# The last projection of an attention and FFN kernel: eight products of blocks replaced by seven (Strassen's scheme in Winograd's form), with the weight forms kept in DRAM

## What is computed

```python
def reference(x, ctx, gate, up, down):           # x, ctx: 16 x 128 x 1024, f32
    q, k, v = layernorm(x), ctx, ctx             # 8 heads over the 128 channels
    kvs = einsum('bnhd,bnhe->bhde', softmax(k, over n), v)
    x = x + einsum('bnhd,bhde->bnhe', softmax(q, over d), kvs)
    h = layernorm(x)                             # 2048 tokens x 1024
    inter = silu(h @ Wg.T) * (h @ Wu.T)          # 2048 x 2752
    return x + inter @ Wd.T                      # 2048 x 1024
```

## Time and profile before

| | us |
|---|---|
| median of the runs | 1581.06 |
| the profiled execution | 1582.67 |
| its span in the profile | 1581.0 |
| PE busy, of the span | 1560.3 (99%) |
| ACT busy | 847.4 (54%) |
| DVE busy | 479.3 (30%) |
| POOL busy | 60.9 (4%) |
| DMA | 203.5 MB, mean 129 GB/s |

### The profile page before, as it was taken

How to read it: one execution, slowest core, us unless ns; L and a number is a source line. 1 busy time by engine, 2 the same in 40 slices (tenths; PEclk the granted TensorE clock), 3 DMA queues, 4 the chain that set the end, 5 groups by cost and what they waited for, 6 DMA issues and landing times.

```text
span 1581.0 us, 17409 instructions
## 1 busy us (share of the span) xinstructions
PE 1560.3 (99%) x7296; PEld 1297.2 (82%) x7296; DVE 479.3 (30%) x592; ACT 847.4 (54%) x865; POOL 60.9 (4%) x99
## 2 busy tenths in 40 slices
PE   7999999999999999999999999999999999999999
PEld 6888788888888888888888888888778888888887
DVE  6998321212212222112122122213422224322221
ACT  5777876666666677666666666773211114111110
POOL 3434000000000000000000000000000000000000
PEclk9999999999999999999999999999999999999999
DMA  6553443333334433333333344336663433443340
GB/s 207 170 171 120 158 124 112 113 103 111 93 104 117 120 114 112 100 114 111 104 111 95 100 120 120 114 104 200 226 235 120 150 138 112 150 144 113 143 148 28
DMA packets 96430, 203.51 MB, mean 129 GB/s; under 512 B 7520, under 2 KB 52576, under 8 KB 92512
## 3 DMA queue, kind: packets, MB, share of 16 engines
q1 hardware_dynamic: 96352, 202.41, 40.6%
HBM read 150.99 MB, written 51.38 MB: 128 GB/s over the span
## 4 chain that ended last, share of the span: by engine, by line
PE 92%; ACT 4%; DMA 2%; issue 1%; SPq 1%; DVE 0%; DVEq 0%; ACTq 0%
PE bank L945 20%; PE bank L946 20%; PE bank L947 20%; PE bank L998 9%; PE bank L1000 9%; PE bank L999 9%; PE bank L896 2%; PE bank L923 1%; PE bank L930 1%; PE bank L913 1%; DMA F<-inter_scratch 1%; ACT early L548 1%; SPq L385 1%; ACT F L582 1%; ACT F L567 1%
## 5 line engine op out<-in xcount | busy, mean ns | idle before, releaser
L945 PE MATMUL bank<-R 128*128 128x512 f32 x1376 | 535.9, 389 | 0.0
L946 PE MATMUL bank<-R 128*128 128x512 f32 x1376 | 535.8, 389 | 0.0
L947 PE MATMUL bank<-R 128*128 128x512 f32 x1376 | 535.7, 389 | 0.0
L527 ACT ACTIVATE F<-F 128x1024 f32<-128x1024 f32 x441 | 467.5, 1060 | 13.3
L947 PEld LDWEIGHTS bank<-R 128*128 128x128 f32 x1376 | 258.4, 188 | 53.6
L945 PEld LDWEIGHTS bank<-R 128*128 128x128 f32 x1376 | 258.4, 188 | 53.4
L946 PEld LDWEIGHTS bank<-R 128*128 128x128 f32 x1376 | 258.4, 188 | 53.4
L663 ACT CAST R<-F 128x2816 fp32r<-128x2816 f32 x30 | 76.7, 2557 | 347.5 <-PE bank L1004 321.7
L998 PE MATMUL bank<-R 128*128 128x512 f32 x642 | 250.2, 390 | 2.6 <-DVE R L844 2.6
L1000 PE MATMUL bank<-R 128*128 128x512 f32 x642 | 250.0, 389 | 0.0
L999 PE MATMUL bank<-R 128*128 128x512 f32 x642 | 250.0, 389 | 0.0
(11 more groups left out here) (75 smaller groups left out, 791.4 us busy)
## 6 DMA issues: line engine op xcount, KB each, us to landing
F<-inter_scratch SPq DMA_DIRECT2D x30, 1408.0 KB, 7.5
inter_scratch<-F SPq DMA_DIRECT2D x84, 256.0 KB, 2.4
F<-in_gu_codes SPq DMA_DIRECT2D x41, 512.0 KB, 3.9
F<-in_gu_scales SPq DMA_DIRECT2D x82, 256.0 KB, 3.9
F<-in_d_codes SPq DMA_DIRECT2D x22, 512.0 KB, 3.8
F<-in_d_scales SPq DMA_DIRECT2D x44, 256.0 KB, 3.9
wd_scratch<-F SPq DMA_DIRECT2D x22, 512.0 KB, 4.5
F<-in_x SPq DMA_DIRECT2D x16, 512.0 KB, 3.6
```

The lines of the kernel that those rows point to most:

```text
L527: nc.scalar.activation(y, y, ACT.Prelu, bias=bias, scale=scale, alpha=alpha).then_inc(bent, 1)
L945: pe.matmul(dst, hi, xh[:, tb, t, :], start=(t == 0), stop=False)
L946: pe.matmul(dst, hi, xl[:, tb, t, :], start=False, stop=False)
L947: i = pe.matmul(dst, lo, xh[:, tb, t, :], start=False, stop=(t == HT - 1))
```

## The change

The down projection for 20 of the 21 full chunks is done in 5 rounds (4 chunks each) of 8 groups (two token tiles each), 40 groups. A group multiplies a 2x2 arrangement of activation blocks A (128 tokens x 256) with a 2x2 arrangement of weight blocks B (256 x 512), and does it with seven products in place of eight. A product is two steps of three matmuls. The operands are four activation blocks or sums of them (S1 to S4) and B blocks or sums (T1 to T4):

```diff
@@ ScalarE, gate and up stage, after each silu_of(c, tb)
+            def form_hi(c, tb):
...
+                wait(act, form_stored, 16 * k)
+                nc.scalar.copy(form[0], src).then_inc(fh_ready, 1)
@@ VectorE, gate and up stage, in every second chunk
+            def t_forms(c):
...
+                sub(T1, B12, B11).then_inc(t_ready, 1)
+                sub(T3, B22, B12).then_inc(t_ready, 1)
...
+                sub(T2, B22, T1).then_inc(t_ready, 1)
...
+                sub(T4, B21, T2).then_inc(t_ready, 1)
@@ VectorE, gate and up stage, after each block_out(c, tb)
+            def form_lo(c, tb):
...
+                dve.wait_ge(fh_ready, k + 1)
+                sub(form[1], src, form[0].bitcast(F32)).then_inc(fl_ready, 1)
@@ SyncE at the turn
             store_block(FULL, 0, HALF)
+            for m in range(NM // 4):
+                load_y(m)
             store_block(FULL, 1, HALF)
...
             store_block(FULL, 3, HALF)
...
+            load_stage(1)
+            for m in range(NM // 4, NM):
+                load_y(m)
...
+            for g in range(NG):
+                r, m = g // NM, g % NM
+                if g + 2 < NG:
+                    load_stage(g + 2)
+                if r + 1 < NR and m < NP:
+                    sp.wait_ge(product_done, NP * r * NM + m + 1)
+                    load_w(r + 1, m)
...
@@ ScalarE, down stage
+            for s in range(2):
+                act.wait_ge(inter_stored[s], 16 * (2 * FULL + 4))
+            for g in range(NG):
+                r, m = g // NM, g % NM
+                snapshot(g, 0, 0, (s3_added, g), s1_ready)
+                if g + 1 < NG:
+                    hi_a(g + 1)
+                if r == NR - 1 and m == 0:
+                    for k in range(2):
+                        act.wait_ge(restw_in, 32)
+                        nc.scalar.copy(restw[k][0], restw_in_f[k]).then_inc(hrw_ready, 1)
+                    hi_rest(0)
+                snapshot(g, 1, 2, (s2_added, g), s2_ready)
+                if g + 1 < NG:
+                    hi_s(g + 1)
+                snapshot(g, 0, 4, (s1_added, g + 1), s3_ready)
...
@@ VectorE, down stage
+                elif g:
+                    x_add(g - 1, (product_done, NP * g))
+                s1_add(g)
+                if g + 1 < NG:
+                    s_forms(g + 1)
+                    lo_a(g + 1)
+                q1_add(g)
+                s2_add(g)
+                if not last:
+                    w_add(g, (product_done, NP * g + 4))
+                if g + 1 < NG:
+                    lo_s(g + 1)
...
+                s3_add(g)
+                if not last:
+                    q2_add(g, (product_done, NP * g + 6))
...
@@ TensorE, down stage
-                        pe.matmul(dst, h, wdh[:, k, :], start=(k == 0), stop=False)
-                        pe.matmul(dst, h, wdl[:, k, :], start=False, stop=False)
-                        i = pe.matmul(dst, l, wdh[:, k, :], start=False, stop=False)
...
+            def product(g, i, dst, stationary, start):
...
+                for k in range(2):
+                    h, l = (v[:, k * P:(k + 1) * P] for v in stationary)
...
+                last.then_inc(product_done, 1)
...
+                pe.wait_ge(la_ready, g + 1)
+                wait(pe, x_added, g - 1)
...
+                product(g, 0, x, a11, True)
+                pe.wait_ge(ls_ready, g + 1)
+                wait(pe, q2_added, g - 1)
...
+                product(g, 1, q, s3, True)
+                pe.wait_ge(s1_ready, g + 1)
...
+                product(g, 2, x, s2, False)
+                wait(pe, w_added, g - 1)
...
+                product(g, 3, w2, a12, True)
+                pe.wait_ge(s2_ready, g + 1)
...
+                product(g, 4, x, s1, False)
+                pe.wait_ge(q1_added, g + 1)
...
+                product(g, 5, q, a22, False)
+                pe.wait_ge(s3_ready, g + 1)
...
+                product(g, 6, x, s4, False)
+                if r == NR - 1:
+                    pe.wait_ge(lrw_ready, 2)
+                    pe.wait_ge(lr_ready, m + 1)
...
+                    rest(m, w2, 0, 0, True)
+                    rest(m, q, 1, 0, True)
+                    rest(m, x, 0, 1, True)
+                    wait(pe, z_added, m)
+                    rest(m, bankZ, 1, 1, False)
```

More of the change, by code:

```diff
@@ L201, in xattn_ffn, with wd_tile @@
[L201 to L203 removed]
+        B11, B12, B21, B22 = [v[:, h * WIDE:(h + 1) * WIDE] for v in wdt for h in range(2)]
+        T1, T2, T3, T4 = tform
+        FORMS = [(B11, 0), (B21, 3), (B22, 6), (T1, 4), (T3, 1), (T2, 2), (T4, 5)]
+        KINDS = (2, 0, 3, 1)
+        def wd_tile(c):
+            return 4 * (c // 4) + KINDS[c % 4] if c < KW else c
@@ L646, in last_block @@
                 nc.scalar.copy(inter[s][0:HALF, :], banks[tb][HALF:P, 0, :]).then_inc(up_copied, 1)
-            def split_weights(half, a=0, b=KT):
-                for k in range(a, b):
-                    for g, (start, _) in enumerate(GROUPS):
-                        if start == k:
-                            act.wait_ge(stage_in[g], 16 * (half + 1))
-                    if half:
-                        act.wait_ge(down_step, KT * (TT - 1) + k + 1)
-                    nc.scalar.copy(wdh[:, k, :], stage[k]).then_inc(wdh_ready, 1)
@@ new lines, in snapshot, with hi_rest @@
+            def snapshot(g, i, product, freed, ready):
+                act.wait_ge(product_done, NP * g + product + 1)
+                wait(act, *freed)
+                nc.scalar.copy(snap[i], bankX[g % 2]).then_inc(ready, 1)
+            def hi_rest(m):
+                act.wait_ge(irest_in[m % 2], 16 * (m // 2 + 1))
+                wait(act, rest_done, 4 * (m - 1))
+                if m == 0:
+                    act.wait_ge(product_done, NP * (NG - NM))
+                nc.scalar.copy(resti[m % 2][:, :, 0:2, :], irest[m % 2]).then_inc(hr_ready, 1)
@@ new lines, in _ @@
+            mixer_turn(LOOPS, XS + 3)
+            for c in range(FULL):
+                n = 2 + 3 * c
+                weigh(n, wdt[c % 2])
+                if c % 2 and c < KW:
+                    t_forms(c)
+                block_out(c, 0)
+                form_lo(c, 0)
+                weigh(n + 1, w[1 - n % 2])
+                dve.wait_ge(w_ready, n + 2)
+                lo_of(c * 2 + 2, 1 - n % 2, 0, (c + 1) % 2)
+                block_out(c, 1)
+                form_lo(c, 1)
+                if c < FULL - 1:
+                    weigh(n + 2, w[n % 2])
+                    dve.wait_ge(w_ready, n + 3)
+                    lo_of(c * 2 + 3, n % 2, 1, (c + 1) % 2)
+                else:
+                    weigh(n + 2, wdt[1])
+                block_out(c, 2)
+                form_lo(c, 2)
+                block_out(c, 3)
+                form_lo(c, 3)
@@ new lines, in _ @@
+            last_block(0)
+            lo_a(0)
+            last_block(1)
+            s_forms(0)
+            last_block(2)
+            dve.wait_ge(gate_done, FULL * TB + TB)
+            lo_s(0)
+            last_block(3)
+            for g in range(NG):
+                r, m = g // NM, g % NM
+                last = r == NR - 1
+                if last and m:
+                    rest_adds(g - 1)
+                elif g:
[10 more added lines that the diff above has]
+                    lo_s(g + 1)
+                if last and m == 0:
+                    for k in range(2):
+                        dve.wait_ge(hrw_ready, k + 1)
+                        sub(restw[k][1], restw_in_f[k], restw[k][0].bitcast(F32)).then_inc(lrw_ready, 1)
+                    lo_rest(0)
+                s3_add(g)
+                if not last:
+                    q2_add(g, (product_done, NP * g + 6))
+                elif m + 1 < NM:
+                    lo_rest(m + 1)
@@ L977, in _ @@
             chunk(0, 0, 1)
-            for p in range(0, PAIRS):
-                for j in range(2):
-                    chunk(p * 2 + (1 + j), 1 - j)
+            for c in range(1, FULL):
+                chunk(c, c % 2)
             for tb in range(TB):
@@ new lines, in rest @@
+            def rest(m, dst, t, h, onto):
+                cols = slice(h * WIDE, (h + 1) * WIDE)
+                hi, both, lo = (resti[m % 2][:, t, i, :] for i in range(3))
+                pe.matmul(dst, hi, restw[0][0][:, cols], start=not onto, stop=False, skip_group_check=onto)
+                pe.matmul(dst, hi, restw[0][1][:, cols], start=False, stop=False, skip_group_check=onto)
+                pe.matmul(dst, lo, restw[0][0][:, cols], start=False, stop=False, skip_group_check=onto)
+                pe.matmul(dst, both, restw[1][0][:, cols], start=False, stop=False, skip_group_check=onto)
+                pe.matmul(dst, both, restw[1][1][:, cols], start=False, stop=True, skip_group_check=onto).then_inc(rest_done, 1)
```

591 lines of the change are left out of this document (292 added, 299 removed).

## The result

The changed kernel takes **1540.27 us** (median of four runs, 1539.45 to 1540.83); the kernel before took 1581.17 us beside it (four runs). The ratio is 0.9736, with a 95% interval of 0.9719 to 0.9753. The forecast was 1540, range 1530 to 1561. The profiled execution lasted 1539.45 us, its span 1537.7 us.

What follows compares the result with a forecast made beforehand. The down stage was taken as paced by TensorE's number of matmuls. Terms summed to −41.1 us against the profiled 1582.7, giving 1541.6; with the runs' median 1.6 below that execution, the forecast was 1540, range 1530 to 1561.

Steps and rivals of the forecast that it cites:

- Matmuls: Down stage: 1840 matmuls, 240 fewer than before, saving 54.4 us and leaving 416.9 us.
- The gate and up stage: Stage before the down stage: added copies, differences and stores of forms stay hidden, costing 0.
- The old pauses: Earlier kernel's down stage: pauses go with the loads that made them, saving 3.5 us.
- (b): Start of down stage: first snapshot waits until the last activations are stored, delaying the third product, +3.2 us.
- The clock: Start of down stage: a pause of 9 us brings TensorE's half clock, +1.5 us (0 to 3.4).
- (c): Start of down stage: third group's load queues behind six of residuals, delaying the second group's fifth product, +9.3 us.
- the turn costs little: Rival, start of down stage: queue serves the third group's small load beside the residuals, some 11 us back, 1530; chance 0.09.
- (d): Start of down stage: `q1_add` stands behind the third group's sums and split on VectorE, +0.3 us.
- Last round: Last round's first group: extra casts and `hi_rest` on ScalarE, two splits on VectorE before `rest`, +1.1 us.
- VectorE, 8.6 us a group: Down stage: VectorE's instructions sum to 8.6 us per group, 7.6 to 9.0 with spacing, within the group's 9.52.
- The late snapshots: Rival, down-stage groups: `hi_s` delays ScalarE's snapshots 0.5 us beyond cover, about 64 us, giving 1604; chance 0.05.
- The end: End of the kernel: last store is 512 KB instead of 256 and follows another, +1.3 us.

Runs made afterwards that it cites:

- e12: Changed kernel with early loads moved ahead, residuals one per group, first snapshots and second group's activations in own memory, last round's splits spread: 1525.38 us.
- e10: The kernel before, with the weights of its second half asked for in small lots between the tiles instead of all at once: 1580.05 us.
- e7: e4 with the low part of the 128x1024 split made three times per group, 2.5 us more for VectorE: 1558.29 us.
- e1: Changed kernel with the third group's load of activations asked for before the six loads of residuals: 1533.56 us.
- e11: The changed kernel run again, unedited: 1540.90 us.
- e2: Changed kernel with the first group's snapshots in memory of their own, so they wait for no store: 1541.12 us.
- e4: e3 with the residuals asked for one load per group: 1531.69 us.
- e3: Changed kernel with the edits of e1 and e2 together: 1534.12 us.
- e6: e4 with the low part of the 128x768 split made twice per group, 0.98 us more for VectorE: 1541.26 us.
- e8: e4 with the four sums of token blocks made on POOL instead of VectorE: 1534.62 us.

## Why the prediction was right

Its mechanism held: the stage is still paced by the number of matmuls. Point by point:

- **Matmuls, −54.4.** Shown by e12: with every wait gone the stage is within 0.6 us of 416.9.
- **The gate and up stage, 0.** From 200 to 1000 us TensorE is busy 800 of 800 us after as before, with VectorE at 224 us instead of 162 and ScalarE at 571 instead of 538.
- **The old pauses, −3.5.** They were 3.3 (474.7 less 471.3) and went, but half of the cause was wrong. The prediction put both waits of the earlier trace rows down to the weights in the queue; e10 shows that the first isn't. It stood behind the split of a whole tile in one piece, as its rows above show; that it disappeared because such splits did is argued, no run tests it.
- **(b) the first snapshot, +3.2.** Third product at T+6.15 instead of T+2.97: +3.2.
- **The clock, +1.5.** There were two slow stretches. The one after the first pause took 4.22 us for 11 matmuls that need 2.49, +1.7; the second 3.82 us for 9 that need 2.04, +1.8. The sum had only the second. It was not wrong by the first, since the second pause absorbs it: TensorE reached its fifth product at T+20.2 and waited 6.8 us instead of the 9.3 of (c). So the clock dipped twice, where "once" was written. The prediction's sentence on the Trainium skill ("TensorE: Matmul & The Clock Gate", section "HAM oscillation — how this bites in real kernels") said that pause (b) might also pay, and the trace shows it do so: 0.50 after 3.0 us. But it doesn't bear the sentence out as a rule: in e7 a pause of 3.1 us before the first group's fifth product left the clock at 1.00.
- **(c) the third group's load, +9.3.** Split at T+25.7 where T+26 was taken, product at T+27.1 where T+27.5 was. So 1.7 + 6.9 = 8.6 stands for 9.3. e1 gave back 7.3 us of this and its slow clock. The rival "the turn costs little" is out: the small load came only 17.8 us after its issue behind the large ones, and moving it ahead of them took that pause away.
- **(d) +0.3**: no such wait is listed, 0. **Last round, +1.1**: it cost 1.6, of which the list has the wait of 0.9; e12 gained 1.6.
- **VectorE, 8.6 us a group** was too high. The independent steps start 0.07 us before the last one ends in most places, so the group has 7.8 (sums 0.42 where 0.41 was estimated). 82%, not nine tenths, and at the low end of both bounds given.
- **The late snapshots** didn't occur: in the steady groups there is no wait of TensorE for L717.
- **The end, +1.3**: 0.6.

Within the stage the prediction had 0.1 + 3.2 + 9.3 + 0.3 + 1.1 + 1.5 = 15.5 us beside the matmuls, and the profile 15.8; about 1 us of these is spread over small distances that no long wait names. That the two sums agree within 0.3 us is partly luck: (c) was too large by 0.7 and (d) by 0.3, the last round too small by 0.5, and the same kernel profiled again (e11) had 16.7, because the second slow stretch lasted to 1134.7 there. Stage and end together gave −41.4 against the sum's −41.1; that 1540 is within 0.3 us of the median is closer than the medians of one kernel are to each other (1540.27 and 1540.90).

What the prediction didn't see is the second group's load under the first pause (e2 to e4). It had no effect on the forecast but on every edit of the turn: (b), (c) and the clock were priced at 14.0 us together, and e3 gave back 6.8.

## What to carry to other kernels

When a stage is paced by one engine, count its instructions for the gain and walk the first groups for the cost: of the 15.8 us above the matmuls, 13.9 were at one turn and went with the order and place of a few small loads and copies. Pauses that end at a fixed landing absorb what lies ahead of them, so remove them from the last backwards, and look what waits beneath before you price the first. Slack isn't one minus the busy share: e6 lost a fiftieth of each group with VectorE still idle for a tenth of it, because the slack ahead of the one add that frees a bank was gone.

## What was not expected of the hardware

- **A bank that comes free just late costs more than its lateness.** In e6 TensorE started 0.05 us late and lost 0.2 us per group, in the pitch of the next two matmuls (0.33 and 0.24 instead of 0.227). The list of waits shows 0.2 us for the whole stage where 7.8 were lost.
- **The clock and short pauses.** Idle times of 2.9 (e1), 3.0 (after), 3.1 (e4) and 6.8 us (after) each had the granted clock at about half for 3 to 4 us of the work behind. One of 1.2 us (e1) left it at 1.00, and so did one of 2.5 us and, at 1113.5, one of 3.1 us in e7:

```profile
1114.00:1116.00 2.00, 1.95 (x9) 1.27 (x8) 2.00 (x4) 1.37 (x2) 0.00 (x0) 1.00 1.03 422
```

So the length of a pause alone doesn't decide. Nor does it say how long the clock stays low: it was at 0.50 for nearly 7 us in e3 (behind 3.2 us) and in e8 (3.8 us), for half of that in e4 (3.1 us), and for 5.6 us of the work behind the second pause in e11 against 3.5 in the first profile of the same kernel. Why was not tried; the 0.9 us by which the two profiles of the unedited kernel differ are this.
